# First chunk of the shared network moved into the gate as plain fp32 products, and the last stage's product stream started at the second chunk

## The chip, the core and the metric

The kernel runs as one program on one core of a Trainium2 chip. The core has a matrix engine (TensorE, in the profile PE for its products and PEld for its weight loads), a vector engine (DVE), an activation engine (ACT), GpSimd (POOL), and a queue engine (SP) that here issues the DMA transfers. They run beside each other, each its own instructions in order, and wait for one another through semaphores. The metric is the device time of one execution in microseconds (us), as the median of several runs.

## What is computed

Four layers follow one another, each added to its input `x` of shape (16, 256, 256): attention, a gated linear recurrence (minGRU), a mixture of experts with a shared network, and a tanh recurrence over the 256 positions. The last two are what the change touches:

```python
# layer 3: experts, two of four chosen per batch row, and the shared network
gate_scores = softmax(gate(mean(x)) * (1 + scale) + shift)      # 16 x 4
out = sum over the chosen e of w[b, e] * mask[e] * (gelu(x @ ew1[e] + eb1[e]) @ ew2[e] + eb2[e])
shared = gelu(x @ sw1 + sb1) @ sw2 + sb2                        # sw1 256x1024, sw2 1024x256
x = x + out + shared
# layer 4: tanh recurrence over time
h = tanh(x[:, t] @ Wx + b + h @ Wh)                             # 256 steps, each after the other
x = x + h
```

`shared` reads only the `x` that enters layer 3. It is needed position by position in layer 4, since step t takes `x[:, t]` as layer 3 left it.

## The kernel before

The state is kept transposed in SBUF as `XT` (128 partitions of features, 2 halves, 16 batch rows, 256 positions). The kernel has four stages, each a block of its own for all engines: no engine enters a stage before all have left the one ahead.

**Attention** (`attention`, L130, 0 to about 453 us). Beside it, SP and POOL prepare the weights of the four experts and of the shared network for later: 40 pieces are loaded into `modw`, split on POOL into a rounded part and a remainder (`wparts`, L231 and L233), and written to DRAM as `weight_halves` (L225). A split weight allows fp32-like products of fp32r type: a product is then three matrix products (high by high, high by low, low by high).

**Gated recurrence** (`recurrence`, L842, about 453 to 574 us). TensorE's products here (L887) are plain fp32.

**Experts** (`experts`, L1017, about 574 to 977 us). First the gate: DVE reduces `XT` over the positions (L1125), makes `prod` and `prod2` (L1134, L1137), TensorE sums them over the partitions with a matrix of ones (L1262, L1264), and a chain of small DVE operations with one exponential on ACT (L1111) yields the chosen experts (`which`). SP reads them and issues the loads of the chosen weights into `w1` and `w2` (L1042, L1046), two jobs ahead. Then come 32 jobs (16 batch rows, two experts each) of 8 ticks: `up` (6 products, L1280 to L1282) into `ph`, gelu on ACT (L1118), split of the result on DVE (L1226, L1228), `down` (6 products, L1296 to L1298) into `py`, two ticks behind. Before the first `up`, TensorE has nothing but the 8 gate products.

**Shared network and tanh recurrence** (`shared_and_rnn`, L1310, about 977 us to the end). The 256 positions are 16 chunks of 16 positions; with 16 batch rows a chunk has N = 256 columns. The shared network of a chunk is FFN = 96 products (8 column blocks of 128 hidden features, 6 up and 6 down products for each), called items here. They form one stream that a generator (`all_ffn`) hands out, chunk after chunk. Before, the order on TensorE is written out so: all 96 items of chunk 0; the bias rows of the recurrence (L1455); AHEAD = 14 items of chunk 1; then for each step k the recurrent products `recur` (L1392, with `wh_sb`), every second step the input products `drive` (L1403, with `wx_sb`) for the two steps to come, and `quota(k)` items of the stream, 5 on even and 7 on odd steps, and EXTRA more of them on each of the first EXTRA_STEPS steps. One step is: TensorE `recur`, DVE transpose (L1499), ACT tanh (L1474), TensorE again. The gelus (L1483), splits (L1507, L1509) and the addition of a finished chunk to `XT` (`add_x`, L1516) are put behind the step that the same count of items gives (`step_of`), each engine in that order. POOL clears `hs` (L1534) and forms the output chunks in `staged` (L1543), which SP sends (L1559).

These lines set the order on TensorE in the last stage:

```python
work = all_ffn()
for _ in range(FFN):            # chunk 0
    next(work, None)
...                             # bias rows of the recurrence
for _ in range(AHEAD):
    next(work, None)
drive(0)
for k in range(T):
    recur(k)
    if k % 2 == 0 and k // 2 + 1 < PAIRS:
        drive(k // 2 + 1)
    for _ in range(quota(k)):
        next(work, None)
```

## Time and profile before

| | us |
|---|---|
| median of 3 runs | 1357.46 (1354.88 to 1358.3) |
| the profiled execution, its own time | 1354.25 |
| its span in the profile | 1352.5 |
| TensorE products, busy | 1215.1 (90%) |
| DVE / ACT / POOL, busy | 883.2 (65%) / 632.5 (47%) / 329.9 (24%) |
| stages, from the timeline | attention to 453, gated recurrence to 574, experts to 977, last stage to the end |

The profile gives each instruction's start and duration on its engine, and where an engine was idle, what ended the wait. PEclk is the clock that TensorE was granted, as a share of full speed: 1.00 is 2.4 GHz, 0.50 is 1.2 GHz. A plain fp32 product is shown as two records.

### The profile page before, as it was taken

How to read it: one execution, taken by the hardware profiler on the slowest of the kernel's cores; microseconds unless marked ns; L12 is line 12 of the kernel's file. 1: busy time of each engine (PE TensorE's matmuls, PEld its weight loads, DVE VectorE, ACT ScalarE, POOL GpSimd, SP SyncE). 2: the span in 40 equal slices, each digit the busy share in tenths (PEclk: the TensorE clock that was granted, in tenths of full speed). 3: DMA queues.
4: the chain of work that ended last, by engine and by line, in shares of the span. 5: the costliest groups of instructions: out<-in, count | busy, mean ns of one | idle time of the engine just before them, and what ended most of it. 6: DMA issues, size and time to landing. Idle time of an engine off the chain costs nothing. (4 is left out here: it accounts for less than half of the span.)

```text
span 1352.5 us, 34667 instructions
## 1 busy us (share of the span) xinstructions
PE 1215.1 (90%) x14232; PEld 977.0 (72%) x14232; DVE 883.2 (65%) x2091; ACT 632.5 (47%) x1191; POOL 329.9 (24%) x311
## 2 busy tenths in 40 slices
PE   4389999999998888329999999999999999999995
PEld 2257676766665333129999999999988888888884
DVE  4978787887864399867666666666555555555552
ACT  2167777777766599612333333333233333333331
POOL 1554544444453299800000000000000000000000
PEclk9799999999999899759999999999999999999996
DMA  9212121211214000039999999999700000000000
GB/s 348 94 48 95 48 95 49 85 59 64 80 49 148 24 0 1 0 129 397 397 374 366 364 364 365 367 365 364 273 2 18 10 19 11 19 10 19 11 18 18
DMA packets 81196, 188.31 MB, mean 139 GB/s; under 512 B 4112, under 2 KB 14480, under 8 KB 80784
## 3 DMA queue, kind: packets, MB, share of 16 engines
q1 hardware_dynamic: 81040, 186.11, 38.1%
q8 instruction: 113, 1.85, 0.6%
q14 instruction: 43, 0.35, 0.1%
HBM read 160.66 MB, written 25.17 MB: 137 GB/s over the span
## 5 line engine op out<-in xcount | busy, mean ns | idle before, releaser
L1118 ACT ACTIVATE g<-ph,b 128x256 f32<-128x256 f32 x256 | 121.2, 474 | 248.3 <-PE ph L1282 248.3
L549 DVE TENSOR_REDUCE mx<-pR 128x4 f32<-128x1024 f32 x128 | 156.3, 1224 | 62.6 <-PE pR L707 61.2
L1499 DVE STREAM_TRANSPOSE preT<-pr 128x64 f32<-128x64 f32 x256 | 63.7, 249 | 163.7 <-PE pr L1392 163.2
L1280 PE MATMUL ph<-xhi,w 128*128 128x256 f32 x512 | 145.8, 285 | 13.2 <-DMA w<-weight_halves 13.2
L1226 DVE CAST ghi<-g 128x256 fp32r<-128x256 f32 x256 | 74.7, 292 | 126.6 <-ACT g L1118 126.4
L1474 ACT ACTIVATE hs<-preT 128x32 f32<-128x32 f32 x256 | 58.7, 229 | 199.6 <-DVE preT L1499 198.6
L1296 PE MATMUL py<-ghi,w 128*128 128x256 f32 x512 | 145.7, 285 | 1.7 <-DVE glo L1228 1.6
L1281 PE MATMUL ph<-xlo,w 128*128 128x256 f32 x512 | 145.7, 285 | 0.0
L1282 PE MATMUL ph<-xhi,w 128*128 128x256 f32 x512 | 145.7, 284 | 0.0
L1297 PE MATMUL py<-glo,w 128*128 128x256 f32 x512 | 144.9, 283 | 0.0
L1298 PE MATMUL py<-ghi,w 128*128 128x256 f32 x512 | 144.9, 283 | 0.0
L421 ACT ACTIVATE probs<-pR 128x1024 f32<-128x1024 f32 x128 | 129.3, 1024 | 22.6 <-PE pR L716 21.0
L1392 PE MATMUL pr<-wh_sb,hs 128*32 128x64 f32 x4096 | 114.0, 231 | 8.9 <-ACT hs L1474 8.9
L1228 DVE TENSOR_TENSOR glo<-g,ghi 128x256 fp32r<-128x256 f32 x256 | 108.9, 425 | 8.8
L1280 PEld LDWEIGHTS ph<-xhi,w 128*128 128x128 f32 x512 | 99.1, 193 | 13.5 <-issue 13.5
L1543 POOL TENSOR_TENSOR staged<-xc,hs 128x256 f32<-128x256 f32 x32 | 22.7, 732 | 347.5 <-ACT hs L1474 347.5
L1392 PEld LDWEIGHTS pr<-wh_sb,hs 128*32 128x32 f32 x4096 | 71.4, 112 | 46.1 <-ACT hs L1474 13.4
L887 PE MATMUL pg<-XT,wfih_sb 128*128 128x512 f32 x192 | 86.4, 600 | 17.1 <-DVE pn L979 15.9
L1296 PEld LDWEIGHTS py<-ghi,w 128*128 128x128 f32 x512 | 98.2, 192 | 3.4 <-DVE glo L1228 3.2
L1534 POOL MEMSET hs<- 128x2048 f32 x1 | 1.8, 1804 | 403.0 <-POOLq L1049 403.0
L1281 PEld LDWEIGHTS ph<-xlo,w 128*128 128x128 f32 x512 | 99.1, 194 | 0.0
L1282 PEld LDWEIGHTS ph<-xhi,w 128*128 128x128 f32 x512 | 99.1, 194 | 0.0
(195 smaller groups left out, 2973.0 us busy)
## 6 DMA issues: line engine op xcount, KB each, us to landing
w<-weight_halves SPq DMA_DIRECT2D x132, 1024.0 KB, 7.9
weight_halves<-wparts SPq DMA_DIRECT2D x40, 512.0 KB, 3.9
modw<-in_ew SPq DMA_DIRECT2D x32, 256.0 KB, 4.6
xn<-in_x_tok SPq DMA_DIRECT2D x4, 1024.0 KB, 11.7
XT<-in_x_dm SPq DMA_DIRECT2D x2, 2048.0 KB, 14.8
out_dm<-staged SPq DMA_DIRECT2D x16, 256.0 KB, 2.1
modw<-in_sw SPq DMA_DIRECT2D x8, 256.0 KB, 4.0
modw<-in_mod_w SPq DMA_DIRECT2D x1, 768.0 KB, 7.0
```

The costliest lines, as they stand in the source:

```text
L421: nc.scalar.activation(probs[:, j % 4], pR[k][:], ACT.Exp, scale=HD ** -0.5).then_inc(free[k], 1)
L549: nc.vector.reduce_max(mx[:, :, 2 * j:2 * j + 2].rearrange("p t s -> p s t"), pR[k][:].rearrange("p s (t k) -> p s t k", t=TC), AX.X).then ...
L887: i = nc.tensor.matmul(pg[n % 2][:, g], wfih[:, c, g * D + u * P:g * D + (u + 1) * P], XT[:, c, 2 * p:2 * p + 2], start=(c == 0), stop=(c ...
L1118: nc.scalar.activation(g[:, t % RING], ph[t % RING][:, 0:T], ACT.Gelu_apprx_tanh, bias=b1[:, n, f:f + 1]).then_inc(gelu_done, 1)
L1228: nc.vector.tensor_tensor(glo[:, t % RING], g[:, t % RING], ghi[:, t % RING].bitcast(fp32), ALU.subtract).then_inc(lo_done, 1)
L1280: nc.tensor.matmul(dst, whi, hi, start=(k == 0), stop=False)
L1281: nc.tensor.matmul(dst, whi, lo, start=False, stop=False)
L1282: i = nc.tensor.matmul(dst, wlo, hi, start=False, stop=(k == DC - 1))
L1296: nc.tensor.matmul(dst, whi, hi, start=(f == 0), stop=False)
L1297: nc.tensor.matmul(dst, whi, lo, start=False, stop=False)
L1298: i = nc.tensor.matmul(dst, wlo, hi, start=False, stop=(f == FC - 1))
L1392: i = nc.tensor.matmul(dst[QW * j:QW * (j + 1)], prev[:, c], quad(wh[:, c], j), start=False, stop=(c == DC - 1), skip_group_check=True)
```

## The change

1. `wfih_sb` is kept through the whole program, and two buffers `raw1` and `raw2` (8 KB a partition each) are added behind the attention stage. In the gated recurrence SP loads the unsplit `sw1` and `sw2` into them (1 MB each). To make their place free, SP waits at the end of attention until the last `weight_halves` are written.
2. In the experts stage TensorE computes chunk 0 of the shared network from `raw1`, `raw2` and `XT` with plain fp32 products: 6 `first_up` and 2 `first_down` (two products each) ahead of the gate products, 2 `first_up` and 6 `first_down` behind them, ahead of the wait for the expert weights. ACT does 6 gelus ahead of the exponential, 2 behind it, with table loads between, and copies the result from PSUM to `y0` (in `raw1`).
3. The gate's products move to another PSUM buffer, and several scratch tiles are placed inside `wfih_sb`, `wx_sb` and `wh_sb`. SP therefore loads `wx_sb` and `wh_sb` only after the gate products.
4. In the last stage the stream has chunks 1 to 15. TensorE starts with 14 items of chunk 1, the bias rows and `drive(0)`. DVE adds `y0` to `XT` for chunk 0 at the stage's start. EXTRA goes from 2 to 3, EXTRA_STEPS from 8 to 10. POOL's order of clearing is changed, and DVE waits for `hs` to be clear.

Cut to its core (renamed views, index shifts from `FC * c` to `FC * (c - 1)` and scratch tiles are left out):

```diff
@@ attention, end of SP's program
             sp.wait_ge(max_moved, 32 * B)
+            for q in range(2):
+                sp.wait_ge(env["pieces_out"][q], 16 * (PIECES // 2))
@@ recurrence
+        @block.sync
+        def _(sp):
+            sp.dma_start(env["raw1"][:], env["sw1"].rearrange("(c p) n -> p c n", p=P)).then_inc(env["shared_in"], 16)
+            sp.dma_start(env["raw2"][:], env["sw2"].rearrange("(c p) n -> p c n", p=P)).then_inc(env["shared_in"], 16)
@@ experts, SP
+                sp.wait_ge(gate_mm, 1)
                 for dst, src in ((wx_sb, "wx"), (wh_sb, "wh")):
@@ experts, ACT
+                def first_gelu(f):
+                    act.wait_ge(up_first, f + 1)
+                    if f >= RING:
+                        act.wait_ge(down_first, f - RING + 1)
+                    nc.scalar.activation(g[:, f % RING], ph[f % RING][:, 0:T], ACT.Gelu_apprx_tanh,
+                                         bias=vec("sb1", f, f + 1)).then_inc(gelu_first, 1)
+                for f in range(EARLY):
+                    first_gelu(f)
+                nc.scalar.preload_act_table_set("natural_log_exp_and_others")
                 act.wait_ge(exp_in, 1)
                 nc.scalar.activation(lg[:], lg[:], ACT.Exp).then_inc(exp_done, 1)
+                for f in range(EARLY, FC):
+                    first_gelu(f)
+                act.wait_ge(down_first, FC)
+                nc.scalar.copy(y0, py[0][:, :, 0:T]).then_inc(y_kept, 1)
@@ experts, TensorE
+                def first_up(f):
+                    if f >= RING:
+                        pe.wait_ge(gelu_first, f - RING + 1)
+                    for k in range(DC):
+                        i = nc.tensor.matmul(ph[f % RING][:, 0:T], raw1[:, k, f * P:(f + 1) * P], XT[:, k, :, 0:CH],
+                                             start=(k == 0), stop=(k == DC - 1))
+                    i.then_inc(up_first, 1)
+                def first_down(f):
+                    pe.wait_ge(gelu_first, f + 1)
+                    for m in range(DC):
+                        i = nc.tensor.matmul(py[0][:, m, 0:T], raw2[:, f, m * P:(m + 1) * P], g[:, f % RING],
+                                             start=(f == 0), stop=(f == FC - 1))
+                    i.then_inc(down_first, 1)
+                pe.wait_ge(env["shared_in"], 32)
+                for f in range(EARLY):
+                    first_up(f)
+                    if f >= EARLY - 2:
+                        first_down(f - EARLY + 2)
                 pe.wait_ge(gate_in, 1)
...
                 i.then_inc(gate_mm, 1)
+                for f in range(2, FC):
+                    if EARLY + f - 2 < FC:
+                        first_up(EARLY + f - 2)
+                    first_down(f)
@@ shared_and_rnn
-    AHEAD, EXTRA, EXTRA_STEPS = 14, 2, 8
+    AHEAD, EXTRA, EXTRA_STEPS = 14, 3, 10
@@ shared_and_rnn, TensorE
-                for c in range(NCH):
+                for c in range(1, NCH):
                     yield from ffn(c, (slice(None), slice(0, B), slice(CH * c, CH * (c + 1))))
...
-            for _ in range(FFN):
+            for _ in range(AHEAD):
                 next(work, None)
             pe.wait_ge(row1_set, 1)
...
-            for _ in range(AHEAD):
-                next(work, None)
             drive(0)
@@ shared_and_rnn, DVE
             for k in range(-1, T):
                 if k >= 0:
                     recur(k)
                 for c in adds_in[k]:
-                    if k >= 0:
-                        add_x(c)
+                    add_x(c)
+                if k < 0:
+                    add_x(0)
+                    bias_of_state()
                 for c, f in splits_in[k]:
                     split(c, f)
-                    if (c, f) == (0, FC - 1):
-                        add_x(0)
-                        bias_of_state()
```

**TensorE at the gate.** In the order of instructions, `ph` and `py` are PSUM buffers, `raw` the unsplit weights; one row here is one product, two records in the profile. Before:

```order
L1257 UNCONDITIONAL_BRANCH [waits barrier_Pool_Activation_PE_DVE_SP_release]
L1262 MATMUL ph<-prod,ones 128x64 [waits tables,gate_in]
L1262 MATMUL ph<-prod,ones 128x64 x5
L1264 MATMUL ph<-prod,ones 128x128 x2
L1280 MATMUL ph<-xhi,w 128x256 [waits w1_in00,x_split,exp_in]
```

After (the rows behind these are the second group of early products, 4 up and 12 down in all):

```order
L1293 MATMUL ph<-XT,raw 128x256 [waits shared_in]
L1293 MATMUL ph<-XT,raw 128x256 x7
L1293 MATMUL ph<-XT,raw 128x256 [waits gelu_first]
L1293 MATMUL ph<-XT,raw 128x256
L1300 MATMUL py<-g,raw 128x256 [waits gelu_first]
L1300 MATMUL py<-g,raw 128x256
L1293 MATMUL ph<-XT,raw 128x256 [waits gelu_first]
L1293 MATMUL ph<-XT,raw 128x256
L1300 MATMUL py<-g,raw 128x256 [waits gelu_first]
L1300 MATMUL py<-g,raw 128x256
L1312 MATMUL py<-wx_sb,ones 128x64 [waits tables,gate_in]
L1312 MATMUL py<-wx_sb,ones 128x64 x5
```

16 early products now stand between the stage's start and the gate products.

**DVE at the start of the last stage.** `gs` or `raw` is the gelu's output, `ghis` and `glos` its two parts. Before, the stage opens with 8 pairs like the first two rows (chunk 0), then comes what follows here:

```order
L1509 TENSOR_TENSOR glos<-gs,ghis 128x256 [waits hi_ok]
L1516 TENSOR_TENSOR xc<-XT,pys 128x16x16 [waits staged_done0,down_ok]
L1516 TENSOR_TENSOR xc<-XT,pys 128x16x16
L1490 COPY hs<-small 128x2x16 [waits zeroed]
L1492 COPY bias_tile<-pr 128x64 [waits bias_rows]
```

After, from the stage's first instruction:

```order
L1540 UNCONDITIONAL_BRANCH [waits barrier_Pool_Activation_PE_DVE_SP_release]
L1572 TENSOR_TENSOR xc<-XT,raw 128x16x16 [waits staged_done0]
L1572 TENSOR_TENSOR xc<-XT,raw 128x16x16
L1544 COPY hs<-small 128x2x16 [waits zeroed]
L1546 COPY bias_tile<-pr 128x64 [waits bias_rows]
L1549 COPY pr<-bias_tile 128x64 [waits bias_kept]
L1549 COPY pr<-bias_tile 128x64
L1561 CAST ghis<-raw 128x256 [waits down_ok,gelu_ok]
L1563 TENSOR_TENSOR glos<-raw,ghis 128x256 [waits hi_ok]
L1561 CAST ghis<-raw 128x256 [waits down_ok,gelu_ok]
L1563 TENSOR_TENSOR glos<-raw,ghis 128x256 [waits hi_ok]
L1553 STREAM_TRANSPOSE preT<-pr 128x64 [waits step_done] x2
```

The eight pairs are gone; the addition and the bias copies are first, and two pairs of chunk 1 still stand ahead of the first transpose.

## Rows read from the trace of the kernel before

**Rows 1.** Busy us and counts by engine, granted clock, DMA share: steady last stage.

```profile
1100.00:1200.00 100.00, 100.00 (x2160) 83.40 (x2160) 54.22 (x192) 32.97 (x109) 7.11 (x10) 1.00 0.05 16
```

**Rows 2.** Timeline of the start of the last stage, TensorE and POOL: start, duration.

```profile
977.95 0.47 PE L1414 MATMUL phs<-xhi,w 128*128 128x256 f32 x1 [1.75 <-SPq L1555]
980.57 0.41 PE L1414 MATMUL phs<-xhi,w 128*128 128x256 f32 x1
991.33 0.43 PE L1455 MATMUL pr<-small,row 128*32 128x64 f32 x16
977.52 1.80 POOL L1534 MEMSET hs<- 128x2048 f32 x1 [402.98 <-POOLq L1049]
```

**Rows 3.** Timeline of the same place, DVE.

```profile
992.40 0.21 DVE L1492 COPY bias_tile<-pr 128x64 f32<-128x64 f32 x1
992.64 0.35 DVE L1495 COPY pr<-bias_tile 128x64 f32<-128x64 f32 x2
993.23 0.29 DVE L1507 CAST ghis<-gs 128x256 fp32r<-128x256 f32 x1 [0.23 <-ACT gs L1483]
994.63 0.24 DVE L1499 STREAM_TRANSPOSE preT<-pr 128x64 f32<-128x64 f32 x1
```

**Rows 4.** Stretches of 1 us at that place, columns as in rows 1.

```profile
977.00:978.00 1.00, 0.05 (x1) 0.08 (x1) 0.24 (x1) 0.00 (x0) 0.48 (x1) 1.00 0.00 0
978.00:979.00 1.00, 1.00 (x5) 1.00 (x6) 0.00 (x0) 0.00 (x0) 1.00 (x1) 0.52 0.08 16
981.00:982.00 1.00, 1.00 (x8) 1.00 (x8) 0.65 (x2) 0.39 (x2) 0.00 (x0) 0.77 0.00 0
```

**Rows 5.** Timeline, DVE transposes: with extra items, steady, and with an empty stream.

```profile
1000.79 0.25 DVE L1499 STREAM_TRANSPOSE preT<-pr 128x64 f32<-128x64 f32 x1 [1.12 <-PE pr L1392]
1004.05 0.25 DVE L1499 STREAM_TRANSPOSE preT<-pr 128x64 f32<-128x64 f32 x1 [1.12 <-PE pr L1392]
1315.87 0.25 DVE L1499 STREAM_TRANSPOSE preT<-pr 128x64 f32<-128x64 f32 x1 [0.89 <-PE pr L1392]
1318.64 0.25 DVE L1499 STREAM_TRANSPOSE preT<-pr 128x64 f32<-128x64 f32 x1 [0.89 <-PE pr L1392]
1331.11 0.25 DVE L1499 STREAM_TRANSPOSE preT<-pr 128x64 f32<-128x64 f32 x1 [0.78 <-PE pr L1392]
1332.40 0.25 DVE L1499 STREAM_TRANSPOSE preT<-pr 128x64 f32<-128x64 f32 x1 [1.04 <-PE pr L1392]
```

**Rows 6.** Timeline of the gate and the first expert job, all engines.

```profile
573.97 8.98 DVE L1125 TENSOR_REDUCE segs<-XT 128x16 f32<-128x1360 f32 x6 [3.03 <-PEq L849]
584.87 2.83 PE L1262 MATMUL ph<-prod,ones 128*128 128x64 f32 x12 [29.30 <-DVE prod L1137]
588.69 0.23 DVE L1141 TENSOR_TENSOR lg<-ph,small 128x64 f32<-128x64 f32 x1 [3.88 <-PE ph L1264]
595.96 0.68 SPq L1042 DMA_DIRECT2D w<-weight_halves  x1
601.89 0.55 PE L1280 MATMUL ph<-xhi,w 128*128 128x256 f32 x1 [13.24 <-DMA w<-weight_halves]
603.59 1.28 ACT L1118 ACT_TABLE_LOAD   x1 [13.16 <-PE ph L1282]
606.20 0.19 PEld L1296 LDWEIGHTS py<-ghi,w 128*128 128x128 f32 x1 [0.43 <-DVE glo L1228]
```

**Rows 7.** Timeline, TensorE in attention: plain fp32 products of 256 columns.

```profile
437.36 1.99 PE L769 MATMUL pR<-oT,wout 128*128 128x256 f32 x8
448.63 3.43 PE L769 MATMUL pR<-oT,wout 128*128 128x256 f32 x8 [0.72 <-issue]
```

**Rows 8.** The end of attention, one stretch, columns as in rows 1.

```profile
443.00:444.00 1.00, 0.84 (x8) 0.00 (x0) 0.00 (x0) 0.12 (x1) 0.00 (x0) 0.50 0.01 2
```

**Rows 9.** Timeline, DVE where a chunk is added in the steady last stage.

```profile
1302.15 1.04 DVE L1516 TENSOR_TENSOR xc<-XT,pys 128x256 f32<-128x256 f32 x2
1303.69 0.24 DVE L1499 STREAM_TRANSPOSE preT<-pr 128x64 f32<-128x64 f32 x1
```

More of the change, by code:

```diff
@@ L121, in vec @@
             return small[:, at + (a or 0):at + (width if z is None else z)]
-        with ExitStack() as early:
-            wfih_sb = sb(early, "wfih_sb", [P, DC, 3 * D])
-            attention(nc, locals())
-            recurrence(nc, locals())
+        wfih_sb = sb(hold, "wfih_sb", [P, DC, 3 * D])
+        shared_in = sem(hold, "shared_in")
+        attention(nc, locals())
+        raw1 = sb(hold, "raw1", [P, DC, F])
+        raw2 = sb(hold, "raw2", [P, FC, D])
+        recurrence(nc, locals())
         experts(nc, locals())
@@ L1022, in experts @@
     JOBS = TOP * B
+    EARLY = 6
     TICKS = JOBS * FC
@@ L1034, in experts @@
         wxh_in = sem(st, "wxh_in")
+        raw1, raw2 = env["raw1"], env["raw2"]
+        y0 = raw1[:, :, 0:T]
+        up_first, gelu_first, down_first, y_kept = (sem(st, n) for n in ("up_first", "gelu_first", "down_first", "y_kept"))
         def load_weights(sp, n, src, up, down):
@@ L1054, in experts @@
             agg = sb(routed, "agg", [P, 3, DC, B])
-            prod = sb(routed, "prod", [P, 3 * DC, B, NE])
-            prod2 = sb(routed, "prod2", [P, DC, B, 2 * NE])
+            prod = wx_sb[:].rearrange("p c n -> p (c n)")[:, 0:3 * DC * B * NE].rearrange("p (k b e) -> p k b e", k=3 * DC, b=B)
+            prod2 = wh_sb[:].rearrange("p c n -> p (c n)")[:, 0:DC * B * 2 * NE].rearrange("p (k b e) -> p k b e", k=DC, b=B)
             ones = sb(routed, "ones", [P, P])
@@ L1062, in experts @@
             red = sb(routed, "red", [P, B])
-            gt = sb(routed, "gt", [P, B, NE, NE])
-            eq = sb(routed, "eq", [P, B, NE, NE])
+            room = env["wfih_sb"][:].rearrange("p c n -> p (c n)")
+            gt, eq = (room[:, a:a + B * NE * NE].rearrange("p (b e o) -> p b e o", b=B, e=NE) for a in (0, B * NE * NE))
             rank = sb(routed, "rank", [P, B, NE])
@@ L1156, in _ @@
                 other = lg[:].unsqueeze(2).broadcast_to([P, B, NE, NE])
[L1157 to L1158 removed]
+                s.op(nc.vector.tensor_tensor(gt, other, mine, ALU.is_gt))
+                s.link(nc.vector.tensor_tensor(eq, other, mine, ALU.is_equal))
                 dve.wait_ge(tables, 5 + NE)
[L1160 to L1162 removed]
+                s.link(nc.vector.tensor_tensor(eq, eq, earlier[:].unsqueeze(1).broadcast_to([P, B, NE, NE]), ALU.mult))
+                s.link(nc.vector.tensor_tensor(gt, gt, eq, ALU.add))
+                s.link(nc.vector.reduce_sum(rank[:], gt, AX.X))
                 s.op(nc.vector.tensor_scalar(sel[:, :, 0], rank[:], 0.5, None, ALU.is_lt))
@@ L1354, in step_of @@
             at = -1
-            taken = FFN + AHEAD
+            taken = AHEAD
             while taken < end:
@@ L1423, in ffn @@
                         f = n - 2
-                        pe.wait_ge(lo_ok, FC * c + f + RING + 1)
-                        if f == 0 and later(c):
+                        pe.wait_ge(lo_ok, FC * (c - 1) + f + RING + 1)
+                        if f == 0:
                             pe.wait_ge(x_ready, c)
@@ L1440, in all_ffn @@
             def all_ffn():
-                for c in range(NCH):
+                for c in range(1, NCH):
                     yield from ffn(c, (slice(None), slice(0, B), slice(CH * c, CH * (c + 1))))
```

54 lines of the change are left out of this document (27 added, 27 removed).

## Prediction

> **What bounds the kernel now.** I read first which engine fills the last stage, then what stands ahead of its first step, then the gate, and last the places where the change adds a wait. In the steady last stage TensorE is busy 100 of 100 us at full clock, while DVE has 54 and ACT 33 [rows 1]. So there a step costs what TensorE has to do in it, and no wait of another engine shows. Two steps take 2.77 us (from 1315.87 to 1318.64) [rows 5], with 12 items of the stream. With 16 items (7 and 9, while EXTRA counts) they take 3.26 us (from 1000.79 to 1004.05) [rows 5]. An item thus costs 0.12 us. When the stream is empty a step is a chain of TensorE, DVE and ACT, and takes 1.29 us at half clock (from 1331.11 to 1332.40) [rows 5].
>
> The stage's first product starts at 977.95 [rows 2], the first transpose only at 994.63 [rows 3]: 16.68 us in which no step of the recurrence is done. Most of it is chunk 0, 96 items. The gate is the other place: TensorE waits 29.3 us ahead of the gate products and 13.2 us behind them for the expert weights [rows 6]. There chunk 0 can be computed for nothing, if it delays neither the gate nor the first job.
>
> **What the last stage gains.** After the change the 14 items of chunk 1 come first. At the stage's start items follow one another every 0.218 us (twelve items from 977.95 to 980.57) [rows 2], half clock by the granted clock of that stretch [rows 4]. 14 x 0.218 = 3.05 us. The bias rows take 0.43 us at full clock [rows 2]; I take 0.6 here, since part of them may be at half clock. DVE has long added chunk 0 (1.04 us [rows 9]), and POOL has cleared `hs` 1.80 us after 977.52, with two small clears ahead of it now [rows 2], so neither is late: both are done before 979.8. The copies of the bias take 0.59 us (from 992.40 to 992.64 + 0.35) [rows 3]. The two splits that still stand ahead of the first transpose take 1.40 us (from 993.23 to 994.63) [rows 3]. The new `drive(0)` and `recur(0)` lie beside them. With 0.1 us for signals the sum is 3.05 + 0.6 + 0.59 + 1.40 + 0.1 = 5.75 us in place of 16.68: **10.9 us less**.
>
> **What the last stage gives back.** The stream behind the first step has the same length as before (1,426 items), but EXTRA takes 30 items early in place of 16. These 14 cost 14 x 0.12 = **1.7 us** while TensorE is the bound. They come off the end: counting the quotas, the last item falls in step 232 in place of 235. Each of these three steps becomes an empty one, 1.29 in place of 1.39 us: **0.3 us less**. It does not repay, since the empty step is bound by its chain.
>
> Counting also shows one tight place. In the first chunk of the stream the up products of block 7 end in step 7, its gelu comes in step 7, its split in step 8 behind the transpose, and its down products are the fifth item of the same step 8. Before, they came in step 10. The split ends 0.25 + 0.72 us and two signals after the recurrent products of step 8; TensorE has `drive` and 4 items, about 0.7 us, to fill it. I take **0.45 us** more for this stall, between 0 and 0.7. In all later chunks (15 chunks of 96 items against 16 steps of 96 items, so one pattern) every split has at least a whole step. Last stage: -10.9 + 1.7 - 0.3 + 0.45 = -9.05 us.
>
> **What the gate costs or gains.** The nearest rows of a plain fp32 product of 256 columns are the projections of attention: 4 of them, 8 records, take 1.99 us in one place and 3.43 us in another at lower clock [rows 7]. That is 0.43 us (0.50 with the drain) or 0.86 us for each. Ahead of the gate products stand 16 of them. TensorE comes from idleness, so it starts at half clock; in the last stage it went from half to full clock about 3.5 us after its first product [rows 2, 4], in the stretch that shows 0.77. So 4 us at half clock for 4 to 5 products, then 11.5 x 0.43 = 5: done some 9 us after 573.97, at 583, while the gate products start at 584.87 because DVE is busy with its reduction and what follows it [rows 6]. Cover: 1.9 us. If the clock never rose, 16 x 0.86 = 13.8 us, and the gate would be 2.9 us late. ACT follows: a gelu is a short operation beside four buffers in the ring, and its loads of tables lie ahead of the first product's end and ahead of the exponential. I cost them at nothing; the cover is the DVE chain.
>
> The gate products with their drain take 3.82 us at half clock (from 584.87 to 588.69) [rows 6]. If the early products leave the clock at full speed, they would take half, 1.9 us less, and the expert weights would be asked for that much earlier. The row against it: in the stage change at 976 the clock was full, TensorE idled 1.75 us, and was at half speed when it began again [rows 2, 4]. The gap here is about the same. I take half, **0.95 us less**, and keep 0 and 1.9 as ends.
>
> A rule of the Trainium skill bears on this gap (page "TensorE: Matmul & The Clock Gate", section "Why this matters for your kernels"): it asks to avoid idle gaps that are well longer than this one, so by it the clock would stay full and the gain would be the whole 1.9 us. The trace does not agree for the gap of 1.75 us ahead of the last stage.
>
> Behind the gate products stand 16 more products, 6.9 to 13.8 us, against 601.89 - 588.69 = 13.2 us of waiting for weights [rows 6]. Only at half clock throughout would they be late, by 0.6 us. The expert weights are issued at 595.96 and this does not move against the gate; `wx_sb` and `wh_sb`, now behind the gate products in SP's queue, go out some 7 us ahead of it and are half a megabyte. Nothing but the last stage reads them. ACT has loaded the gelu's table long before the first expert tick, so the load of 1.28 us in that tick goes. TensorE's weight load waited 0.43 us for the first split there [rows 6]: **0.45 us less**, no more, for only the wait was on the path.
>
> **Free edits.** SP's wait at the end of attention: in the stretch from 443 to 444 the transfers are already still (0.01) [rows 8], 10 us before the stage ends, so nothing waits for it. If the last pieces did land late, all engines would. The 2 MB of raw weights are issued with 120 us to go and nothing else on the queue. Where the scratch tiles lie changes no duration.
>
> **The sum.** -9.05 - 0.95 - 0.45 = -10.45 us. On the profiled execution's own 1354.25 (span 1352.5 and 1.75 around it) that is 1343.8. That execution was 3.2 us below the median of the runs shown, so I put the forecast on the median: 1357.46 - 10.45 = **1347.0 us**.
>
> **Rivals.**
> *A. The early products delay the gate.* The clock stays at half speed or a gelu is late: the gate comes 2.9 us and the first job up to 3.5 us late, no gain of clock. -9.05 - 0.45 + 3.5 = -6.0: 1351.5. For it: TensorE is cold at the start. Against: the last stage's clock rose in 3.5 us with products as dense. Chance 0.10.
> *B. The clock stays low in the first steps.* The short first burst is followed by a pause for the bias copies; if the clock stays at half for 3.4 us more, half of that is lost: -8.8, 1348.7. It lies inside the main case's range. Chance 0.12.
> *C. Each chunk's border stalls TensorE.* The stream now stands differently against the steps; `add_x` falls behind an odd step, with the bias copy. Before, the addition of 1.04 us put the next transpose 1.54 us behind its own start without idling TensorE [rows 1, 9]. If the new place cost a split's wait of 0.72 us at 14 borders, the gain would be gone: -10.45 + 10.1, 1357.1, no difference. Chance 0.04. If the whole addition of 1.04 us were exposed at each, it ends slower: -10.45 + 14.6 = +4.1, 1361.6; it decides from 1.04 us a border. Against both: the split now has more time, not less. Chance 0.02.
> *D. It does not do what it says:* the early products are there but something else of equal length holds the first step, such as `hs` or the weights `wx_sb`. Both are in place long before. Chance 0.02, about 1356.
>
> **Chances and range.** The forecast has 0.70, A 0.10, B 0.12, C 0.06, D 0.02. About 0.3% (4.1 us) is what a measurement of this kernel can tell from no change. Faster by more: 0.92; within: 0.06; slower: 0.02. The range takes in A and the ends of the unknown terms: gate -1.9 and no stall at step 8 give 1345.6, a first burst at full clock (1.5 us less) 1344.1, and the runs before spread by 1 to 2.5 us. So 1342.5 to 1352.0.
>
> **What would show it.** In the new profile: the first transpose 5 to 7 us after the last stage's first product; about 9 us of plain products ahead of the gate products, which start as far behind the stage's start as before (10.9 us); their duration, 3.8 or near 2 us; no table load in the first expert tick; 22.2 us for 16 steps in the steady stage; the last item in step 232; one wait of TensorE near step 8. It is wrong if the time between first and last transpose grows by more than 2.5 us, or if the expert stage's first product comes later after the stage's start than 27.9 us.

## The result, and the profile after

The changed kernel takes **1345.72 us** (median of 4 runs, 1344.65 to 1346.87), the kernel before 1357.88 beside it (4 runs, 1354.88 to 1363.12). The ratio is 0.9899 with a 95% interval of 0.9877 to 0.9922, or 13.7 us less (10.6 to 16.7); the two medians themselves are 12.2 us apart, inside that interval. The forecast was 10.45 us less, 1347.0, and the measured time lies in its range. The profiled execution of after took 1345.54 us, with a span of 1343.7.

The start of the last stage after, TensorE, in a timeline (start, duration, then idle time ahead and what ended it). It answers to [rows 2].

```profile
979.77 0.36 PE L1470 MATMUL phs<-xhi,w 128*128 128x256 f32 x1 [1.72 <-SPq L1610]
...
980.09 0.28 PE L1474 MATMUL phs<-xhi,w 128*128 128x256 f32 x1
...
981.42 0.28 PE L1472 MATMUL phs<-xlo,w 128*128 128x256 f32 x1
981.64 0.43 PE L1511 MATMUL pr<-small,row 128*32 128x64 f32 x16
982.77 0.43 PE L1459 MATMUL pr<-wx_sb,xc 128*32 128x64 f32 x16 [0.70 <-DVE pr L1549]
```

DVE at the same place, which answers to [rows 3], and behind the three dots the transposes of steps 8 to 10:

```profile
979.41 1.06 DVE L1572 TENSOR_TENSOR xc<-XT,raw 128x256 f32<-128x256 f32 x2 [0.32 <-SPq L1607]
981.44 0.18 DVE L1544 COPY hs<-small 128x32 f32<-128x32 f32 x1 [0.96 <-POOL hs L1592]
982.13 0.23 DVE L1546 COPY bias_tile<-pr 128x64 f32<-128x64 f32 x1 [0.52 <-PE pr L1511]
982.66 0.28 DVE L1561 CAST ghis<-raw 128x256 fp32r<-128x256 f32 x1
983.98 0.24 DVE L1553 STREAM_TRANSPOSE preT<-pr 128x64 f32<-128x64 f32 x1
...
997.47 0.25 DVE L1553 STREAM_TRANSPOSE preT<-pr 128x64 f32<-128x64 f32 x1 [1.24 <-PE pr L1448]
999.58 0.25 DVE L1553 STREAM_TRANSPOSE preT<-pr 128x64 f32<-128x64 f32 x1 [1.23 <-PE pr L1448]
1001.36 0.25 DVE L1553 STREAM_TRANSPOSE preT<-pr 128x64 f32<-128x64 f32 x1 [1.26 <-PE pr L1448]
```

The first transpose stands 4.21 us behind the stage's first product (16.68 before). Stretches of that place and of the steady stage (busy us and counts of PE, PEld, DVE, ACT, POOL, granted clock, DMA share, GB/s) answer to [rows 4] and [rows 1]:

```profile
976.00:977.00 1.00, 1.00 (x10) 0.95 (x8) 0.70 (x2) 0.23 (x1) 0.00 (x0) 1.00 0.00 0
980.00:981.00 1.00, 1.00 (x10) 1.00 (x10) 0.47 (x2) 0.23 (x1) 1.00 (x1) 1.00 0.00 0
1100.00:1200.00 100.00, 100.00 (x2161) 83.54 (x2161) 52.56 (x187) 33.11 (x107) 5.71 (x8) 1.00 0.05 16
```

TensorE idled 1.72 us ahead of the stage, about as before (1.75), but began again at full clock: here, the items follow one another every 0.12 us and not every 0.218. The steady stage is what it was, TensorE full and nothing else near it.

The gate after, TensorE, which answers to [rows 6]:

```profile
578.93 6.76 PE L1293 MATMUL ph<-XT,raw 128*128 128x256 f32 x20 [18.41 <-PEq L854]
...
586.39 1.03 PE L1293 MATMUL ph<-XT,raw 128*128 128x256 f32 x4
587.26 1.03 PE L1300 MATMUL py<-g,raw 128*128 128x256 f32 x4
589.84 1.55 PE L1312 MATMUL py<-wx_sb,ones 128*128 128x64 f32 x12 [1.55 <-DVE wh_sb L1166]
591.22 0.66 PE L1314 MATMUL py<-wh_sb,ones 128*128 128x128 f32 x4
...
594.32 4.48 PE L1300 MATMUL py<-g,raw 128*128 128x256 f32 x20
605.00 0.55 PE L1334 MATMUL ph<-xhi,w 128*128 128x256 f32 x1 [6.20 <-DMA w<-weight_halves]
```

Both groups of plain products lie in what was idle time. The first is done 9.36 us after the stage's start (588.29), 1.55 us ahead of the gate products; the second 6.20 us ahead of the first expert product. Both waits still have the same enders as before, DVE and the weights' DMA. The clock rose inside the first group, and the gate products ran at full clock; the stretches show it:

```profile
582.00:583.00 1.00, 1.00 (x4) 0.77 (x3) 1.00 (x1) 0.28 (x1) 0.00 (x0) 0.50 0.00 0
583.00:584.00 1.00, 1.00 (x5) 0.86 (x4) 1.00 (x2) 0.19 (x1) 0.00 (x0) 0.80 0.00 0
590.00:591.00 1.00, 1.00 (x10) 1.00 (x11) 0.00 (x0) 0.16 (x1) 0.00 (x0) 1.00 0.00 0
```

**Where the time went**, by distances between marks in the traces. For each kernel: first expert product after the gate stage's start; gate products to the DVE read behind them; expert stage (first product to the last stage's first item); from there to the first transpose, called T0 from here on; steps 0 to 16, 16 to 224; step 224 to the end of the span (good to 0.05 us, since the span is rounded); and the last stage as a whole. The variants are described under Experiments.

```
                start..expert  gate  experts   T0    0-16   16-224  224-end  last stage
before              27.92      3.82  376.06  16.68  23.80   289.12   44.95    374.55
before_again        27.77      3.82  376.05  16.68  23.80   289.12   44.90    374.50
before_third        27.77      3.82  376.03  15.37  23.80   289.14   44.79    373.10
after               26.07      2.08  374.77   4.21  25.82   288.87   45.03    363.93
after_again         26.06      2.09  374.77   4.21  25.80   288.87   45.06    363.94
e1_extra2           25.95      2.08  374.76   4.22  23.63   289.12   44.46    361.43
e2_no_early         27.72      3.82  376.02   4.22  25.69   288.87   45.11    363.89
e4_gate_only        26.01      2.09  374.77  15.35  23.80   289.12   44.69    372.96
e6_table_back       25.96      2.09  376.04   4.21  25.79   288.87   44.61    363.48
e10_coef_early      26.12      2.08  374.10   5.57  25.73   288.87   44.41    364.58
e3_bias_first       26.11      2.09  375.15   3.20  25.70   288.86   44.99    362.75
e8_all_behind       29.83      3.79  374.22   4.21  25.71   288.88   45.10    363.90
e5_late_raw         25.98      2.09  374.75   4.21  25.78   288.87   45.00    363.86
best                26.11      2.09  374.09   4.07  24.12   289.12   44.49    361.80
```

(In e3_bias_first and best the bias rows come 0.36 us ahead of the first item. Counted to and from them, the expert stage is 374.79 in e3 and 373.73 in best, and T0 is 3.56 and 4.44.)

From before to after: gate 27.92 to 26.07 (with 0.1 of spread, -1.8), experts 376.06 to 374.77 (-1.3), last stage 374.55 to 363.93 (-10.6): **-13.7 us**. That this is the ratio's figure to the tenth is chance. The same sum from before_third, whose last stage began at full clock, is -12.1 us, and what lies ahead of the gate stage is not in it. The two profiled spans differ by 8.8 only, since the gate stage of after's profiled execution began at 578.93 against 573.97, 4.96 us later. The kernel before does the same in other executions (579.88 in before_again, 580.20 in before_third); more on it below.

### The profile page after: what moved, and what is told of

Same layout as the page of the kernel before. It is cut to its first block and busy times, and to the rows that moved or that the text cites. A ratio compares the mean times of both kernels' runs of the same rounds, so it can differ in the third digit from the quotient of the medians.

```text
span 1343.7 us, 34595 instructions
## 1 busy us (share of the span) xinstructions
PE 1223.0 (91%) x14200; PEld 980.4 (73%) x14200; DVE 879.4 (65%) x2075; ACT 637.4 (47%) x1193; POOL 330.5 (25%) x311
## 3 DMA queue, kind: packets, MB, share of 16 engines
q8 instruction: 113, 1.85, 0.6%
## 5 line engine op out<-in xcount | busy, mean ns | idle before, releaser
L1598 POOL TENSOR_TENSOR raw<-xc,hs 128x256 f32<-128x256 f32 x32 | 22.8, 733 | 336.9 <-ACT hs L1528 336.9
L1352 PEld LDWEIGHTS py<-ghi,w 128*128 128x128 f32 x512 | 98.6, 193 | 1.4 <-DVE glo L1258 1.3
L1354 PEld LDWEIGHTS py<-ghi,w 128*128 128x128 f32 x512 | 98.8, 193 | 0.0
## 6 DMA issues: line engine op xcount, KB each, us to landing
xn<-in_x_tok SPq DMA_DIRECT2D x4, 1024.0 KB, 12.1
```

Of the source, the lines that this page charges most:

```text
L1352: nc.tensor.matmul(dst, whi, hi, start=(f == 0), stop=False)
L1354: i = nc.tensor.matmul(dst, wlo, hi, start=False, stop=(f == FC - 1))
```

## Experiments

**The gate part against the last stage.** Three kernels take the change apart. e1_extra2 gives only the extra items back their old number:

```diff
-    AHEAD, EXTRA, EXTRA_STEPS = 14, 3, 10
+    AHEAD, EXTRA, EXTRA_STEPS = 14, 2, 8
```

> The changed kernel with EXTRA 2 on 8 steps, as before: 14 items fewer are taken early. They cost 0.12 us each in steps bound by TensorE, the tight place of step 8 goes (down products of block 7 come in step 10), and the stream ends 3 steps later. Theory: 1.7 + 0.3 - 0.2 = about 1.8 us less than the changed kernel, 1343.9. The rival, that the extra items are needed because the stream now starts cold, expects stalls of TensorE in the first chunk and a time at or over 1345.7.

Measured: 1340.61 us (6 runs, 1338.49 to 1347.07), ratio to before 0.9875 (0.9844 to 0.9905). The expectation was 1343.9. In the traces the last stage is 2.50 us shorter than after's: 2.19 in steps 0 to 16, 0.57 at the end, 0.25 given back between. TensorE's waits from the stage's start to about step 16 are in e1 the same two as in after:

```profile
PE phs L1470 <- SPq L1610: 1.7, 1, 1.7
PE pr L1459 <- DVE pr L1549: 0.7, 1, 0.7
```

(waiting line, what it waited for, us in total, times, longest). So the extra items bought nothing that a missing item would have cost.

The 0.57 us at the end are another matter. There the clock falls to half some us after the last item of the stream, and where it falls differs from trace to trace. Stretches of 1 us around the fall, of after, e1_extra2, before and e10_coef_early in this order (granted clock is the third number from the end):

```profile
1313.00:1314.00 1.00, 0.37 (x20) 0.21 (x20) 0.48 (x2) 0.23 (x1) 0.00 (x0) 0.93 0.00 0
1316.00:1317.00 1.00, 0.59 (x36) 0.43 (x37) 0.25 (x1) 0.23 (x1) 1.00 (x2) 0.73 0.00 0
1326.00:1327.00 1.00, 0.59 (x25) 0.41 (x16) 0.21 (x1) 0.23 (x1) 0.00 (x0) 0.60 0.02 8
1317.00:1318.00 1.00, 0.65 (x32) 0.49 (x32) 0.26 (x2) 0.16 (x2) 0.00 (x0) 0.87 0.00 0
```

By these shares, and by the spans (1343.7, 1340.3, 1352.5 and 1344.1 us), half clock held for the last 29.8, 23.8, 26.3 and 26.4 us. After and e10_coef_early have the same code in the last stage and take 45.03 and 44.41 us from step 224 on, so 0.6 us is the clock alone. At an equal fall, e10_coef_early with EXTRA 3 (44.41) stands against before with EXTRA 2 (44.95): there the extra items give back 0.5 us. An estimate of their net price from these rows is 2.19 - 0.25 - 0.54 = 1.4 us, and not 2.5; no pair of runs shows it by itself.

e2_no_early takes the early products and gelus out and keeps the later start of the stream. It leaves chunk 0 of the shared network out of the result; in its place ACT copies a part of `XT` to `y0`. On TensorE the edit is:

```diff
-                for f in range(EARLY):
-                    first_up(f)
-                    if f >= EARLY - 2:
-                        first_down(f - EARLY + 2)
...
-                for f in range(2, FC):
-                    if EARLY + f - 2 < FC:
-                        first_up(EARLY + f - 2)
-                    first_down(f)
```

> The changed kernel without the early products and their gelus: chunk 0 of the shared network is left out of the sum. If the gate part gains by the clock that the early products leave behind, taking this work out makes the kernel slower: gate products 3.8 us in place of 2.1, a table load of 1.28 us back in the first expert tick (0.45 us), so about 2 us over the changed kernel, near 1347.8. If the early products cost anything that I don't see (contention, a later gate), it is faster than the changed kernel, below 1345.

Measured: 1347.56 us (8 runs), ratio 0.9935 (0.991 to 0.996): with less to do its median is 2.8 us *higher* than that of after beside it (1344.76, ratio 0.9894, 0.9868 to 0.9921). The two intervals overlap, so the whole times alone don't show it; the stages do, with 2.9 us (1.65 to the first expert product, 1.25 behind it). The gate products of this kernel:

```profile
589.17 2.82 PE L1302 MATMUL py<-wx_sb,ones 128*128 128x64 f32 x12 [29.31 <-DVE wh_sb L1161]
...
605.99 0.55 PE L1320 MATMUL ph<-xhi,w 128*128 128x256 f32 x1 [13.04 <-DMA w<-weight_halves]
```

They are at half clock again (3.82 to DVE's read) and start at the same distance, 10.90 against 10.91. So the early products delay nothing, and they are what brings both the gate's gain and, with the gelu's table, the expert stage's.

e4_gate_only is the gate part of the change alone, with the last stage of before (chunk 0 is computed in both places):

```diff
+            for _ in range(FFN):
+                next(work, None)
...
-    AHEAD, EXTRA, EXTRA_STEPS = 14, 3, 10
+    AHEAD, EXTRA, EXTRA_STEPS = 14, 2, 8
```

> One part alone: the gate as changed, with the early products, but the last stage as before, computing chunk 0 itself (96 items, EXTRA 2 on 8 steps). Theory: the gate part by itself gains 1.8 us at the gate and up to 1.3 us in the expert stage, so 1357.9 - 2 to 3 = 1355 to 1356. The rival, that all of the gain is in the last stage, expects 1357.9; the rival that the early work costs expects more than that.

Measured: 1353.51 us (12 runs), ratio 0.9969 (0.9948 to 0.9991), 4.2 us less than before. The stages give -1.8 in the gate and -1.3 with the experts; T0 was 15.35, as in before_third, and not 16.68, which is the clock at the stage's start and not the edit. Gate part and stream part thus add up: -3.1 (e4_gate_only) and -10.7 (e2_no_early against before).

**What shortened the expert stage.** The forecast had 0.45 there, the trace shows 1.29. e6_table_back makes ACT load the other table set again behind the copy of the early result, so that the first expert tick has its load back, as in before:

```diff
                 nc.scalar.copy(y0, py[0][:, :, 0:T]).then_inc(y_kept, 1)
+                nc.scalar.preload_act_table_set("natural_log_exp_and_others")
                 act.wait_ge(b1_ready, 1)
```

> The changed kernel with one load of the exponential's table put behind the copy of the first chunk's result, where ACT is idle, so that the gelu's table must be loaded again in the first expert tick, as in the kernel before. My prediction priced that load at 0.45 us, TensorE's wait for the first split. The trace after says more: the expert stage is 1.29 us shorter, and the first job is paced by DVE, whose first split stands 2.22 us behind the first product in place of 3.50. Theory: DVE is the bound of the first job, so the whole 1.28 us is on the path, and here the expert stage takes 376.05 us again, 1347.0 in all. The rival, my 0.45 us, expects 375.2 us.

Measured: 1347.14 us (6 runs), ratio 0.9927 (0.9904 to 0.995); expert stage 376.04, to 0.02 us that of before. The whole 1.28 us of the load counts. ACT in this kernel, then DVE:

```profile
608.48 1.28 ACT L1148 ACT_TABLE_LOAD   x1 [5.86 <-PE ph L1337]
609.77 0.84 ACT L1148 ACTIVATE g<-ph,b 128x256 f32<-128x256 f32 x2
...
610.28 0.29 DVE L1257 CAST ghi<-g 128x256 fp32r<-128x256 f32 x1 [6.17 <-ACT g L1148]
```

The first product was at 606.78, the first split 3.50 us behind. In after it is 2.22 us behind (605.00 and the first line here), and DVE then works without a pause:

```profile
607.22 0.29 DVE L1256 CAST ghi<-g 128x256 fp32r<-128x256 f32 x1 [5.01 <-ACT g L1147]
607.55 0.43 DVE L1258 TENSOR_TENSOR glo<-g,ghi 128x256 fp32r<-128x256 f32 x1
607.89 0.22 DVE L1216 TENSOR_TENSOR we<-we,lg 128x64 f32<-128x64 f32 x1
...
609.49 0.29 DVE L1256 CAST ghi<-g 128x256 fp32r<-128x256 f32 x1
609.81 0.43 DVE L1258 TENSOR_TENSOR glo<-g,ghi 128x256 fp32r<-128x256 f32 x1
610.16 0.46 DVE L1227 TENSOR_TENSOR cw<-tmp 128x32 f32<-128x32 f32 x3
```

From the first split on, DVE is full with splits and with the coefficients of the jobs (`coefficients()`, some small operations in each tick), 2.27 us from one split to the next. DVE, not TensorE, sets the pace of the first ticks (TensorE's waits for it stand below), and whatever brings its first split forward comes out whole at the end. e8_all_behind, below, bears this out from another side: TensorE is at full clock there, the first split comes 1.67 us behind the first product, 0.55 less than in after, DVE's spacing is the same, and the expert stage is 0.55 us shorter.

If that is so, coefficients made ahead of the first tick must gain more. e10_coef_early does that:

```diff
                 work = coefficients()
+                for _ in range(4):
+                    next(work, None)
                 for t in range(TICKS):
```

> The changed kernel with the first four of the six parts of the mixing coefficients' computation, 5.3 us of small DVE operations, moved from the first job's ticks to the 5 us in which DVE waits for the first gelu. If DVE is the bound of the first job, TensorE's waits there (1.3 us in its weight loads) go, and the expert stage takes about 373.5 us in place of 374.77. The rival, that TensorE's half clock paces the first job, expects 374.8.

Measured: expert stage 374.10, 0.67 us less than after. That is half of the 1.27 expected. TensorE's weight loads no longer wait for DVE, so something else bounds the rest of the first job there; no run separates what. The first split itself came no earlier (2.33 us behind the first product, since the moved operations ran until then), the second 1.69 us behind it and not 2.27. Waits of PEld in the first 18 to 20 us of the expert stage, kernel before, after and e10_coef_early, in this order:

```profile
PEld py L1296 <- DVE glo L1228: 3.2, 7, 0.8
```
```profile
PEld py L1352 <- DVE glo L1258: 1.3, 4, 0.7
```
```profile
PEld ph L1336 <- ACT g L1147: 0.6, 1, 0.6
```

Its whole time, 1345.0 us (6 runs, ratio 0.9908, 0.9881 to 0.9936), does not show 0.7 us: that is below what these medians tell apart. Its trace shows something else of use. The clock fell to half 0.3 us after its last stage's first product:

```profile
979.52 0.35 PE L1472 MATMUL phs<-xhi,w 128*128 128x256 f32 x1 [1.72 <-SPq L1612]
...
980.04 0.41 PE L1472 MATMUL phs<-xhi,w 128*128 128x256 f32 x1
980.25 0.41 PE L1474 MATMUL phs<-xlo,w 128*128 128x256 f32 x1
```

and T0 is 5.57 there. The forecast, worked out for half clock, was 5.75.

**The order at the last stage's start.** e3_bias_first puts the bias rows ahead of the 14 items, so that DVE's copies run beside the items:

```diff
             work = all_ffn()
-            for _ in range(AHEAD):
-                next(work, None)
             pe.wait_ge(row1_set, 1)
...
+            for _ in range(AHEAD):
+                next(work, None)
             drive(0)
```

> The changed kernel with the bias rows ahead of the 14 first products of the last stage, the order of the kernel before. In the trace after TensorE waits 0.70 us between the bias rows and the first input products, for the two copies of the bias on DVE. With the bias rows first these copies run beside the 14 products. Theory: the first transpose comes 3.5 us behind the first product in place of 4.21, 0.7 us less in all. The rival, that DVE's clearing of the state and its splits pace it anyway, expects 4.2 us.

Measured: first transpose 3.56 us behind the bias rows, against 4.21 us behind the first item in after: 0.65 us less, as expected. The pause of 0.70 us ahead of `drive(0)` is gone. DVE's copies now wait for POOL's clear of `hs` (until 986.51, 1.6 us behind the bias rows), and that chain ends last. In the whole time it is not seen: 1344.75 us (6 runs), ratio 0.9898 (0.9877 to 0.9919).

**Does the amount of early work matter?** e8_all_behind puts all of it behind the gate products (on ACT all eight gelus then follow the exponential, and the table load ahead of it goes):

```diff
-                for f in range(EARLY):
-                    first_up(f)
...
+                for f in range(FC + 2):
+                    if f < FC:
+                        first_up(f)
+                    if f >= 2:
+                        first_down(f - 2)
```

> The changed kernel with all 32 early products behind the gate products, none ahead. Theory: TensorE is at half clock for the gate products again (3.82 us in place of 2.08), and the 32 products, 13.8 us at full clock and some 2 us more for the start at half clock, outlast the 13.1 us in which the expert weights arrive: first expert product about 30.4 us behind the gate stage's start in place of 26.06. 4 us over the changed kernel, about 1349.5. The rival, that the wait behind the gate holds all of the early work, expects 27.8 us and 1347.

Measured: 1350.46 us (6 runs), ratio 0.993 (0.9905 to 0.9956). The first expert product comes 29.83 us behind the stage's start instead of 26.07: the plain products now end last and not the weights:

```profile
593.30 2.79 PE L1305 MATMUL py<-wx_sb,ones 128*128 128x64 f32 x12 [29.37 <-DVE wh_sb L1163]
596.84 4.47 PE L1290 MATMUL ph<-XT,raw 128*128 128x256 f32 x12
...
609.78 2.75 PE L1297 MATMUL py<-g,raw 128*128 128x256 f32 x12
612.18 0.47 PE L1328 MATMUL ph<-xhi,w 128*128 128x256 f32 x1
```

Once the gap behind the gate is full, every further product delays the experts. The split into a group ahead and one behind the gate products is what makes the work free. Of the 3.76 us lost here 0.55 come back, since the experts then begin at full clock (items every 0.12 us from 612.49 on), with an expert stage of 374.22.

**The raw weights.** In after, the gated recurrence took 122.86 us against 120.66 before, and the load of the 2 MB of raw weights lies at its start. e5_late_raw holds that load back to 519.10, in the middle of the stage:

```diff
         def _(sp):
+            sp.wait_ge(kept, 8)
             sp.dma_start(env["raw1"][:], env["sw1"].rearrange("(c p) n -> p c n", p=P)).then_inc(env["shared_in"], 16)
```

> The changed kernel with the load of the raw weights put off until the gated recurrence is half done. If the load disturbed the start of that stage, it takes 120.7 us here; if the stage's length goes by the clock alone, it is 120.7 where the clock rose ahead of the stage and 122.3 or more where it rose behind it, and the early products still start without waiting for the weights.

Measured: 1344.41 us (one run); the gated recurrence is 122.84 us with the load out of the way. Stretches in its first microseconds, of after and of e5_late_raw (the last three columns are granted clock, DMA share, GB/s):

```profile
459.00:460.00 1.00, 1.00 (x2) 0.45 (x2) 0.00 (x0) 0.13 (x1) 0.00 (x0) 0.50 0.97 393
460.00:461.00 1.00, 1.00 (x3) 0.28 (x2) 0.00 (x0) 0.55 (x1) 0.00 (x0) 0.74 0.98 358
```
```profile
458.00:459.00 1.00, 1.00 (x3) 0.48 (x2) 0.00 (x0) 0.04 (x1) 0.00 (x0) 0.50 0.00 0
459.00:460.00 1.00, 1.00 (x2) 0.25 (x2) 0.00 (x0) 0.65 (x1) 0.00 (x0) 0.71 0.00 0
```

The clock is at half in the stage's first microseconds with the DMA full and with it still. Over all traces the length goes with the clock alone: 120.7 us where it was back at full by the stage's start (the three of before, e4, e10, best), 122.3 to 123.0 where it rose 3 to 5 us into it (the eight others). e4, e10 and best have SP's wait and the load where after has them, so neither of the two sets the length by itself. That all three traces of before are short, and only three of eleven of the others, is not explained. TensorE's code in attention, in whose end the clock falls and rises at places that differ from trace to trace, is the same; whether this is chance, or whether the change makes the longer form likelier, stays open. If it did, it would cost up to 1.6 us on average (2.2 us in eight of eleven traces), which the stage sum of 13.7 leaves out.

**Repeats.** after_again, before_again and before_third are the two kernels unchanged.

> The changed kernel once more, on the same chip as the next three, for a second trace. My account: the gate products at full clock and the early start of the last stage's steps are of the change, while the 4.96 us by which the gate stage began later than in the trace of before (2.76 us from attention, 2.20 us from the gated recurrence) are not. Then the median is 1344 to 1347 us, the gate stage's start may move by 3 to 5 us from trace to trace, and the time from it to the first expert product stays at 26.1 us within 1 us. The rival, that the raw weights' load or SP's new wait cost these 5 us, expects the gate stage to begin at 579 us again.

> The kernel before, for a second trace. Theory: where TensorE's clock rises and falls in attention and at the start of the gated recurrence is not set by the kernel, so the gate stage, which began at 573.97 us in the first trace of before and at 577.5 to 582.5 in five traces of the changed kernel and its variants, begins at 575 us or later here too. The rival, that the change delays it, expects 574 us within 1 us. In both the expert stage, from first product to the last stage's first product, takes 376.0 us, and the first 16 steps 23.8 us.

> The kernel before once more, for a third trace. The gated recurrence took 120.7 us in both traces of before and in two of eight of the changed family, 122.3 to 122.9 us in the other six; it is short where the clock rose just ahead of the stage. If that is chance, a third trace of before may show either. If the change is behind it, it is 120.7 again. Expert stage 376.05 and last stage 374.5 in any case.

Measured: 1344.76 (6 runs), 1360.02 and 1358.83 (one run each). The stages repeat to 0.2 us, but for T0 of before, 16.68 twice and 15.37 once (so the last stage of before_third was 373.10 where 374.5 was expected), and for the beginning of the gate stage, 573.97, 579.88 and 580.20.

**All that helped, together.** best is after with e1, e3 and e10.

> Three edits of the earlier runs together on the changed kernel: EXTRA 2 on 8 steps, bias rows ahead of the first 14 products, four parts of the coefficients in DVE's wait of the first job. Their stages by the traces: last stage 2.5 us shorter by the first, 0.8 by the second, expert stage 0.7 by the third. They lie in different places, so the sum of 4.0 us is expected: 1345.2 - 4.0 = 1341.2. If the first two share their gain (both act on the first steps), 1342.

Measured: 1342.25 us (6 runs, 1338.1 to 1346.22), ratio 0.9885 (0.9861 to 0.9908). Expected was 1341.2. Its profiled execution is the fastest of those profiled (span 1337.3), although the clock fell to half 0.7 us into its last stage. The small gains are in the trace, but do not add up: the expert stage is 1.04 us below after's where 0.7 was expected. The last stage, from the bias rows on, is 1.8 us below after's where 3.3 was expected; 0.9 of the missing is the clock. By medians it can't be told from e1_extra2. Its median is 2.5 us below after_again's, that of e1_extra2 4.1 us; the intervals of both overlap with after's.

## Why the prediction was right, and where it was off

**The last stage** was forecast at -9.05 and came at -10.62. The parts:

- *T0* was forecast at 5.75 and was 4.21, from the rows above: 14 items 1.87 us (979.77 to 981.64), bias rows and signal 0.49, copies 0.53, splits 1.32. The last three were forecast at 0.70, 0.59 and 1.40, nearly right. The mis-sized term is the first, 3.05: the clock was full. (For that case the forecast's range allowed 1.5 us; by its own rates it is 3.05 - 14 x 0.12 = 1.4, and 1.2 was measured.) The mechanism was the right one, and e10 shows its price at half clock (T0 5.57). The kernel before has both cases too: 16.68 at half, 15.37 at full. At equal clock the change takes 11.1 us off T0 (16.68 to 5.57, or 15.37 to 4.21), and 10.9 was forecast. The other 1.4 us of the 12.5 between before and after is how the clock stood in one trace each: luck, not the mechanism.
- *Extra items*: steps 0 to 16 became 2.02 us longer, where 1.7 for 14 items and 0.45 for a stall made 2.15. The stall is there: one pair of transposes stands 2.11 us apart (997.47 to 999.58) where its neighbours are 1.75 and 1.78 apart, 0.35 more than they. TensorE shows it where the forecast put it, between the fourth and the fifth item of step 8, a down product that starts 0.40 us behind the one ahead and not 0.12:

```profile
998.01 0.28 PE L1491 MATMUL pys<-ghis,w 128*128 128x256 f32 x1
998.41 0.39 PE L1487 MATMUL pys<-ghis,w 128*128 128x256 f32 x1
```

  The last item fell in step 232 as counted. From step 16 on, -0.25 and +0.08: together -0.17 where -0.3 was forecast. From the first transpose to the end after takes 1.85 us more, to the hundredth what was forecast, and that is luck: e10_coef_early, the same code there, takes 1.14 more than before, with the clock's fall at the end as far from the end as in before. The term taken too small is the end's: -0.25 - 0.54 = -0.8 and not -0.3.
- *The last stage at equal clock* is e10_coef_early against before, 374.55 to 364.58: -9.97, against -9.05 forecast.
- *Rival C* (a stall at each chunk border) is not seen: 288.87 us for 208 steps is 22.22 for 16.
- POOL's clear of `hs` ended later than forecast (981.4 against 979.8; DVE's copy `hs` at 981.44 follows it), and still ahead of the bias rows. Here it costs nothing. In e3 the copies wait for it: with the bias rows first, it is next in line.

**The gate** was forecast at -0.95, half of what a full clock would give, and came at -1.8, the whole of it. The term that failed is the half. It was taken because one gap of 1.75 us, ahead of the last stage, had lost the clock. In all nine traces with products ahead of the gate the clock held over the gap there, 1.45 to 1.85 us. The Trainium skill, page "TensorE: Matmul & The Clock Gate", section "Why this matters for your kernels", tells a reader to avoid only gaps well longer than this one. At the gate all nine traces agree with it. At the last stage's change ten of fourteen do; in before, before_again, e10_coef_early and best the clock fell within 0.7 us of the first product behind a gap of 1.7 us. The one row that the forecast weighed was one of the four. Since the longest gap at the gate (1.85 us, e3_bias_first and e6_table_back) kept the clock and shorter ones here lost it, the length of the gap does not decide it alone; what else does, no run here shows.

**The expert stage** was forecast at -0.45 and came at -1.29. The reasoning that failed is "no more, for only the wait was on the path". The wait of 0.43 us was one of seven for the same producer (3.2 us in total in before's first 18 us of the stage). Here each tick waited for the same engine, so that engine was the bound, and the whole shift of its first operation counted, not the first wait alone. e6 shows it at its full size (1.27 us), e8 with 0.55, and e10 in direction, at half the size expected. Of the load itself: the Trainium skill, page "ScalarE: Activation LUTs", section "What ACT_TABLE_LOAD costs", puts a drain of about the load's own length beside it. Here none is seen: the next operation of ACT comes 0.01 us behind the load's end (608.48 + 1.28 and 609.77), and the stage changes by 1.27, the load alone. ACT had been idle ahead of this load; in after, one stands 0.03 us behind an activation (593.70 for 1.28 us), and there too the next operation comes at once, at 594.99.

**What was costed at nothing.** Rival A (early products delay the gate) fell, since the distance to the gate products is 10.90 in before, 10.91 after, and with it the gelus on ACT cost nothing. The raw load costs nothing by e5. SP's wait at the end of attention is in every kernel with the change and was taken out in none, so its price is not shown beyond what the gate stage's start leaves open. The early products' cover was smaller than forecast, 1.55 against 1.9 us, as they took 9.36 us and not 9. Rival B (half clock into the first steps) was not seen, nor D.

**The sum.** -1.8 - 1.3 - 10.6 = -13.7 us against -10.45. The 3.3 us of difference are the last stage (1.6), the clock in the gate (0.9) and the table load (0.8). Of the last stage's 1.6, the clock at its start gave 1.4 and its earlier fall at the end took 0.6, both by chance; 0.9 is left at equal clock. The spread of what lies ahead of the gate stage was named from the runs before (1 to 2.5 us) and is in fact up to 6 us, in the kernel before as well.

## What to carry to other kernels

Work that has to be done anyway and fits in an idle gap of TensorE can gain twice: it leaves its old place, and it warms the clock for what follows the gap. Move only as much as each gap holds (e8 shows the price of too much in one gap, 3.8 us, of which 0.55 came back), and check what the new order leaves over: here the added extra items, meant to feed the pipeline, cost 2.2 us in the first steps, gave back less than 1 later, and fed nothing. When an operation ahead of a pipeline becomes shorter, count the waits in its whole first round: if each of them is for the same engine, price the shift of that engine, and then look for small side work of it that can be done earlier.

## What the runs showed of the hardware that was not expected

- With the same instructions and the same 1.7 us of idle TensorE at the last stage's start, the granted clock behind it was at full in ten traces and at half in four. Half costs 0.9 us (best against e3_bias_first) to 1.4 (e10_coef_early against after). Executions of one kernel differ in this (before 16.68 twice, before_third 15.37), so a single trace's stage start is worth no more than that. The four at half are all among the six traces whose gated recurrence took 120.7 us.
- The start of the gate stage lay between 574 and 584 us, in the kernel before between 574.0 and 580.2, with the same TensorE code ahead of it in all. Two differences are seen, where the clock rises behind attention's end (120.7 or 122.3 to 123.0 us for the gated recurrence) and the length of attention itself. For a difference of a few us the stages have to be compared, not the spans: two profiled executions showed 8.8 us where 13.7 had been gained.
- A plain fp32 product of 256 columns took 0.43 us at full clock (two products, four records, in 0.87 us from 586.39 to 587.26), three fp32r products 0.36 us. The plain form needs no splits on DVE at all, for a fifth more of TensorE.
